# Attention and FFN block on one Trainium2 core: a VectorE finishing step and a group of transposes change places

## The reference

```python
x = x + xattn(layernorm(x), ctx_768, Wq, Wk, Wv, Wo, bo)
x = x + ffn(layernorm(x), ...)

def xattn(x, context, Wq, Wk, Wv, Wo, bo):      # 8 heads of 64
    q, k, v = x @ Wq, context @ Wk, context @ Wv   # split into heads
    attn = softmax(einsum('bihd,bjhd->bhij', q, k) * 64 ** -0.5)
    return einsum('bhij,bjhd->bihd', attn, v) @ Wo + bo

def ffn(x, gamma, beta, q1, s1, b1, q2, s2, b2):
    h = (x - mean(x)) * rsqrt(var(x) + 1e-5) * gamma + beta
    y = silu(h @ dequant(q1, s1) + b1)             # 256 -> 1024
    return x + 0.5 * (y @ dequant(q2, s2) + b2)    # 1024 -> 256
```

## Time and profile before

| what | value |
|---|---|
| median of three runs | 201.87 us |
| profiled execution, whole / span | 201.96 / 200.2 us |
| PE busy | 187.3 us (94%) |
| PEld busy | 180.1 us (90%) |
| DVE busy | 122.9 us (61%) |
| ACT busy | 121.9 us (61%) |
| POOL busy | 109.6 us (55%) |
| DMA, mean over the span | 54 GB/s, nearly all of the loads in the first 35 us |

### The profile page before, as it was taken

How to read it: one execution, slowest core, us unless ns; L and a number is a source line. 1 busy time by engine, 2 the same in 40 slices (tenths; PEclk the granted TensorE clock), 3 DMA queues, 4 the chain that set the end, 5 groups by cost and what they waited for, 6 DMA issues and landing times.

```text
span 200.2 us, 3855 instructions
## 1 busy us (share of the span) xinstructions
PE 187.3 (94%) x1502; PEld 180.1 (90%) x1502; DVE 122.9 (61%) x262; ACT 121.9 (61%) x227; POOL 109.6 (55%) x135
## 2 busy tenths in 40 slices
PE   6989879789889999999999999999999998998994
PEld 6979669689878999899989999999999998998894
DVE  0487985899859544954495558746683577532341
ACT  2267960499708981787268934894289626754480
POOL 5034993269951957096708861695249544367020
DMA  6999950000000000000000000000000000000101
GB/s 164 318 403 368 260 166 5 2 0 3 0 27 1 29 0 0 29 26 0 3 26 26 3 0 28 29 2 0 26 29 0 3 0 28 28 0 3 49 3 52
DMA packets 9480, 10.72 MB, mean 54 GB/s; under 512 B 2268, under 2 KB 8183, under 8 KB 9335
## 3 DMA queue, kind: packets, MB, share of 16 engines
q1 hardware_dynamic: 8837, 9.70, 14.8%
q10 hardware_dynamic: 626, 0.79, 1.4%
HBM read 8.38 MB, written 2.10 MB: 52 GB/s over the span
## 4 chain that ended last, share of the span: by engine, by line
PE 51%; POOL 18%; DVE 12%; SPq 12%; issue 3%; DMA 1%; ACT 1%; DVEq 0%; ACTq 0%
PE H L785 18%; PE T L773 13%; PE T L797 10%; POOL y_lo L280 5%; SPq L213 4%; SPq L207 4%; PE S L752 4%; PE S L759 3%; POOL x_sb L274 3%; POOL rstd L262 3%; PE S L706 2%; DVE probs L524 2%; DVE smax L522 2%; POOL res_scale L266 2%; DMA vw_lo<-bo_lo 1%
## 5 line engine op out<-in xcount | busy, mean ns | idle before, releaser
L252 POOL TENSOR_TENSOR probs<-probs,rsum 128x616 f32<-128x616 f32 x16 | 19.1, 1217 | 39.9 <-DVE rsum L533 39.9
L280 POOL TENSOR_TENSOR y_lo<-y,y_hi 128x512 fp32r<-128x512 f32 x28 | 37.8, 1362 | 4.9 <-ACT y_hi L394 4.3
L785 PE MATMUL H<-hT_hi,w_hi 128*128 128x256 f32 x128 | 36.8, 288 | 2.2 <-issue 1.8
L797 PE MATMUL T<-w_hi,y_hi 128*128 128x256 f32 x128 | 37.0, 289 | 1.1 <-POOL y_lo L280 0.5
L363 ACT ACTIVATE probs<-probs,rstd 128x616 f32<-128x616 f32 x16 | 12.9, 808 | 40.4 <-DVE probs L524 40.4
L797 PE MATMUL T<-w_hi,y_lo 128*128 128x256 f32 x128 | 35.7, 279 | 0.0
L797 PE MATMUL T<-w_lo,y_hi 128*128 128x256 f32 x128 | 35.7, 279 | 0.0
L785 PE MATMUL H<-hT_hi,w_lo 128*128 128x256 f32 x128 | 35.5, 278 | 0.0
L785 PE MATMUL H<-hT_lo,w_hi 128*128 128x256 f32 x128 | 35.5, 277 | 0.0
L390 ACT ACTIVATE y<-H,vec 128x256 f32<-128x256 f32 x64 | 26.6, 468 | 8.4 <-PE H L785 8.4
L785 PEld LDWEIGHTS H<-hT_hi,w_hi 128*128 128x128 f32 x128 | 24.0, 188 | 3.8 <-issue 2.2
(11 more groups left out here) (115 smaller groups left out, 442.8 us busy)
## 6 DMA issues: line engine op xcount, KB each, us to landing
q_sb<-in_L_ffn_fc_q SPq DMA_DIRECT2D x2, 1024.0 KB, 13.2
out_x<-x_sb SPq DMA_DIRECT2D x16, 128.0 KB, 1.7
x_sb<-in_x SPq DMA_DIRECT2D x7, 256.0 KB, 5.6
s_sb<-in_L_ffn_fc_scales SPq DMA_DIRECT2D x2, 512.0 KB, 11.8
s_sb<-in_L_ffn_fc_scales SPq DMA_DIRECT2D x1, 1024.0 KB, 17.7
wq_sb<-in_L_xattn_Wq SPq DMA_DIRECT2D x1, 512.0 KB, 6.0
wo_sb<-in_L_xattn_Wo SPq DMA_DIRECT2D x1, 512.0 KB, 8.6
wk_sb<-in_L_xattn_Wk ACTq DMA_DIRECT2D x1, 384.0 KB, 4.5
```

Of the source, the lines that this page charges most:

```text
L252: nc.gpsimd.tensor_tensor(p, p, rsum[:, j, :].unsqueeze(2).to_broadcast([P, HEADS, J]), ALU.mult).then_inc(norm_done, 1)
L280: nc.gpsimd.tensor_tensor(y_lo[:, two, :], y[:, two, :], f32(y_hi[:, two, :]), ALU.subtract).then_inc(y_lo_done, 1)
L785: ins = mm(r[:, q * W:(q + 1) * W], wt[:, c, m * P:(m + 1) * P], ht[:, c, :], start=i == 0, stop=i == len(steps) - 1)
L797: ins = mm(o, yt[:, m, j * P:(j + 1) * P], wt[:, m, :], start=m == 0 and i == 0, stop=m == M - 1 and i == 2)
```

## The change

Two things change places. On DVE, `finish_tile(a-2, 0)` for a = 2 to 6 stood ahead of `shift_scores(a, 0)` (at the end of the loop's pass before, and once ahead of the loop); it now stands behind `shift_scores(a, 1)` and ahead of `split_h(a-1)`. On PE, for a = 2 to 6, `h_transposes(a-1)` follows one chunk of `fc2(a-2, 1)` where it followed two; seven chunks stand behind it where there were six. The last pair (a = 7) is as before on both engines. No instruction is added or removed.

```diff
@@ DVE @@
                 make_hn(1)
-                finish_tile(0, 0)
                 for a in range(2, NA):
                     shift_scores(a, 0)
                     shift_scores(a, 1)
+                    if a < LAST:
+                        finish_tile(a - 2, 0)
                     split_h(a - 1)
                     invert_sums(a, 0)
...
                     make_hn(a)
-                    if a < LAST - 1:
-                        finish_tile(a - 1, 0)
                 finish_tile(LAST - 1, 0)
@@ PE @@
                     scores(a, 0)
                     scores(a, 1)
-                    fc2(a - 2, 1, range(2))
+                    fc2(a - 2, 1, range(1))
                     h_transposes(a - 1)
-                    fc2(a - 2, 1, range(2, M))
+                    fc2(a - 2, 1, range(1, M))
```

## The result

| | before | after |
|---|---|---|
| median, fast runs on one chip | 201.91 us (4 runs) | 199.56 us (199.21 to 199.89, 4 runs) |
| ratio, 95% interval | | 0.988 (0.9861 to 0.9899) |
| profiled execution, whole / span | 201.96 / 200.2 | 199.74 / 197.9 |

The kernel is 2.35 us faster, 2.0 to 2.8 by the interval; forecast were 2.5 us and 199.4. Repeated later on another occasion the changed kernel took 199.51 us, ratio 0.9883 (0.9861 to 0.9906). All medians here leave out the rare executions that ran at a low granted clock, such as one of 306.43 us at 0.564.

What follows compares the result with a forecast made beforehand. PE, busy 94% of the span, was taken as near its bound, losing time in gaps behind DVE's queue. 1.29 us in pair 2 plus 0.31 in each of four others made 2.53, giving 199.4 us; 8-in-10 range 198.5 to 200.5.

Steps and rivals of the forecast that it cites:

- the five waits: PE's `h_transposes` waiting for DVE's `probs` in pairs 2 to 6: 2.0 us in total, the longest 1.2.
- E to fc1: From PE's first matmul after both tiles' scores (E) to fc1's start: 4.83 (pair 2) or 3.85 us before, 3.54 forecast.
- the rival on stretched reads of S0: Tile 0's maximum and subtraction take twice as long beside PE's scores: 4.4 us slower, 206.3; chance 0.05.
- point of no change: Duration of tile 0's maximum and subtraction on DVE beyond which the change turns slower: 2.01 us.
- PE's bound at fc1, the first rival: PE's own work, not DVE's queue, sets fc1, at E + 3.20: gain 4.2 us, giving 197.7; chance 0.06.
- the seven chunks, 2.47: PE's fc2 chunks between the transposes and fc1, 0.353 us each: claimed to take 2.47 us.
- PE's wait at fc1: PE free at E + 3.20, DVE ready at E + 3.54: PE waits 0.34 us for `split_h` in each pair.
- PE's part at nothing: `h_transposes` one chunk earlier on PE was given no gain; the whole expected gain was DVE's.
- the path through ACT: ACT's exponential and `scale_h` ahead of `split_h`: first half done at E + 1.97 with two chunks, before E + 2.08.
- My 0.3 as an upper bound: Most that moving `h_transposes` earlier on PE could gain per pair, if ACT were later than reckoned: 0.3 us.
- POOL's room: Time `add_b2` has to spare before `finish_tile` at its new place: 2.88 us in pair 4, 1.90 in pair 2.
- the 17.02 us from fc1 to the next E: PE's stretch from fc1 to the first matmul after the next pair's scores: taken as unchanged at 17.02 us.

Runs made afterwards that it cites:

- POOL's delay test: One more POOL instruction ahead of `add_b2`: in the changed kernel 199.30 us (ratio 0.9879), in the kernel before 207.85 us (1.0303).
- DVE's part alone: Changed kernel with PE's list as before, `h_transposes` behind two chunks of fc2: 200.02 us, ratio 0.9887 to the kernel before.
- PE's part alone: Kernel before with `h_transposes` behind one chunk of fc2, `finish_tile` still ahead of the scores: 202.36 us, ratio 1.0017.
- the two with shifted buffers: Changed kernel with an unused 24-byte buffer behind `hn`: 200.22 us, ratio 0.9914; the same plus one more DVE instruction writing that buffer: 201.68 us, 0.9993.
- both runs that keep DVE's order of before: Kernel before with only `h_transposes` moved to behind one chunk: 202.36 us; kernel before with one more POOL instruction ahead of `add_b2`: 207.85 us.

## Why the prediction was right

**The bound and the mechanism** are as predicted: the five waits were DVE's for POOL, passed on to PE. POOL's delay test shows it from both sides.

**The sum.** E to fc1 was forecast as 3.54 and measured as 3.54 or 3.55 in all five pairs; tile 1's maximum began at E + 0.20, `finish_tile` at E + 1.75 (1.74), `split_h` at E + 2.08 (2.08). Tile 0's subtraction went as fast beside PE's scores (0.80 us) as before, so the rival on stretched reads of S0 falls. (Its point of no change was put at 2.01 us for tile 0's work. That counts four pairs only; with the 1.29 us of pair 2, all five together come to nothing at 1.54 + 0.16 + 2.53 / 5 = 2.21.) PE's bound at fc1, the first rival, was put at E + 3.20; with `finish_tile` out of the way it came out as 3.21 to 3.27. The term that was too small is the seven chunks, 2.47: the first matmul behind the transposes holds PE for 0.20 us to the next start (100.66 to 100.86) and not 0.12, so they take 0.20 + 20 times 0.118 = 2.56, and the bound is 0.35 + 0.36 + 2.56 = 3.27. PE's wait at fc1 was thus 0.27 and not the 0.34 forecast. That wait is a gain still to be had, and not one of this change.

**PE's part at nothing.** Right beside this change, as DVE's part alone shows. The reason given was right too: the path through ACT was due 0.11 us ahead of DVE's queue even with two chunks, and taking 0.34 from that queue brought it out. My 0.3 as an upper bound was not needed.

**POOL's room.** Forecast 2.88 us in pair 4; measured 101.70 - 98.80 = 2.90, from `add_b2` at 97.50 of 1.30 us:

```profile
97.50 1.30 POOL L274 TENSOR_TENSOR x_sb<-x_sb,b_half 128x512 f32<-128x512 f32 x1
```

It took 1.30 us beside DVE's maximum (98.44 to 99.24), and 1.31 in the profile before, where DVE was idle beside it. The rule of the Trainium skill, page "SBUF — State Buffer", section "Who interferes with whom", by which a reduction takes nothing from POOL, agrees with this row. The prediction was wrong that the trace before cannot show it. In the untouched pair 7 the maximum ran beside this row, at no cost to either:

```profile
161.18 1.28 POOL L274 TENSOR_TENSOR x_sb<-x_sb,b_half 128x512 f32<-128x512 f32 x1
```

**What was missed.** I took the 17.02 us from fc1 to the next E as fixed. It was 17.09 to 17.11 in three pairs of four, and the stretch behind pair 7's scores 0.48 shorter. Together these are 0.14 us of gain, inside the spread, but a term that the prediction took as fixed and that isn't. The 2.49 us from E to fc1 and this 0.14, less the 0.33 lost before the first touched pair, are the 2.30 of span. That the offsets of the two profiles partly cancel is luck, and so is part of the closeness of 199.56 to 199.4. PE's part alone was expected to cost 0.08 a pair, and in pairs 3 to 6 it cost 0.15 to 0.26. The same 0.08 at the first matmul behind the transposes gives 1.08 + 0.36 + 2.56 = 4.00, and 4.01 was measured in three pairs. Pairs 2 and 6 fit as well from where their transposes began: 1.97 + 0.36 + 2.56 = 4.89 (4.91 measured) and 1.17 + 0.36 + 2.56 = 4.09 (4.11). In pair 6 that start lies 0.10 later after E because E came sooner. The 24 matmuls of fc2 ahead of the scores ran at 0.113 us there and at 0.118 in pairs 3 to 5, while `finish_tile` waited for POOL until 142.44, E - 0.94, where it began at E - 1.03 in pair 5. So as long as POOL sets DVE's start, the distance from E to fc1 isn't a fixed number of DVE's queue alone.

## What to carry to other kernels

An in-order queue that serves two consumers should not take the step whose input comes last first: see which wait heads the queue that the busiest engine stands behind, and move it to where its input is old. Then count what is left in that queue ahead of the release. Here the same step, moved further to behind `split_h` and the sums, gave 1.8 to 1.9 us more, and only then did the place of the transposes begin to matter. A chain from one start to the next, with distances taken from a pair where nothing waits, forecast the new start to 0.01 us. The same method put PE's own bound 0.07 too low, where a mean over 18 matmuls stood in for the first one behind the transposes, which takes longer.

## What the hardware showed that I had not expected

The matmuls of fc1 and fc2 (256 columns, all at a granted clock of 1.00) ran at one of two distances, 0.113 to 0.114 or 0.118 us from start to start, and kept to one for some 24 in a row, in every profile but the two with shifted buffers. Those of the attention output, of the same shape, ran at 0.120 in every profile (90.77 to 94.24 in 29 steps before). The second half of fc1 in pair 3 took 2.82 us before (87.95 to 90.77) and 2.91 after (86.79 to 89.70):

```profile
87.95 0.37 PE L785 MATMUL H<-hT_hi,w_hi 128*128 128x256 f32 x1
...
90.77 0.28 PE L773 MATMUL T<-vw_hi,pT_hi 128*128 128x256 f32 x1
```

```profile
86.79 0.36 PE L784 MATMUL H<-hT_hi,w_hi 128*128 128x256 f32 x1
...
89.70 0.28 PE L772 MATMUL T<-vw_hi,pT_hi 128*128 128x256 f32 x1
```

The last 96 matmuls ran at 0.118 in the profile before and at 0.1135 in that after: 0.4 us, most of the 0.48 above. That is not the change's doing: they ran at 0.1135 in both runs that keep DVE's order of before, too. Which of the two a piece gets varied from one execution to the next of the same kernel (the changed one was profiled twice). With `hT` and all that lies behind it shifted by the 24 bytes the fast one of fc1 was gone in both kernels tried, by the medians 0.7 us slower in one (200.22 against 199.51) and by the ratios 0.5% in the other (0.9993 against 0.9943; different chips). fc2 changed with it: its pieces of 24 and of 48 matmuls all ran at 0.117 in these two profiles. In the last 48 matmuls of the shifted changed kernel, for one, it was 189.98 to 195.47 in 47 steps, against 189.38 to 194.71 unshifted. So where the operands lie takes part in the distance; which of the moved buffers does it, why 24 bytes do it and 2048 don't, and what chooses between the two distances in an unshifted kernel stay open.
